# An attention and feed-forward layer: turning blocks of 32 by 32 on VectorE instead of whole tiles on TensorE

## The reference

```
q, k, v = split(x @ qkv_w + qkv_b)
local   = softmax over the 128 keys behind each query (q . k / 4) @ v      # per head
pooled  = x averaged over chunks of 8 tokens (64 chunks)
rq, (rk, rv) = x @ rq_w + rq_b, split(pooled @ rkv_w + rkv_b)              # 4 heads of 16
lat_out = softmax over earlier chunks (rq . rk / 4) @ rv
remote  = lat_out @ rout_w + rout_b                                        # 256 wide, 16 heads of 16
gate    = sigmoid(local @ gl_w + remote @ gr_w)                            # one number per token and head
mixed   = gate * local + (1 - gate) * remote
x1      = layernorm(x + mixed @ out_w + out_b)
xn      = x1 / (rms(x1) + 1e-8);  h = gelu(xn @ ternary(w_up).T)
out     = layernorm(x1 + h / (rms(h) + 1e-8) @ ternary(w_down).T)
```

## Time and profile before

| | us |
|---|---|
| three runs | 1149.62, 1155.28 (median), 1156.93 |
| profiled execution | 1154.15 |
| its span, first to last instruction | 1152.4 |
| busy: TensorE, VectorE, POOL, ScalarE | 1019.2, 902.5, 698.0, 682.4 |

### The profile page before, as it was taken

How to read it: one execution, slowest core, us unless ns; L and a number is a source line. 1 busy time by engine, 2 the same in 40 slices (tenths; PEclk the granted TensorE clock), 3 DMA queues, 4 the chain that set the end, 5 groups by cost and what they waited for, 6 DMA issues and landing times.

```text
span 1152.4 us, 37627 instructions
## 1 busy us (share of the span) xinstructions
PE 1019.2 (88%) x15616; PEld 642.4 (56%) x15616; DVE 902.5 (78%) x2119; ACT 682.4 (59%) x1076; POOL 698.0 (61%) x874
## 2 busy tenths in 40 slices
PE   5878999999999999999999999999999999986855
PEld 2445565655556565655656565565656555564533
DVE  6688888887887988787888888788788878875445
ACT  2425666656666665666666565666666566664523
POOL 7216675656667576566757565566756565673744
PEclk9889999999999999999999999999999999996877
DMA  7740604325060423416061331616042250600000
GB/s 219 204 125 14 193 21 120 87 77 148 32 193 23 145 61 104 121 42 182 24 167 56 113 94 59 166 33 187 28 131 77 85 139 33 174 23 20 2 19 18
DMA packets 46662, 108.18 MB, mean 94 GB/s; under 512 B 7542, under 2 KB 26486, under 8 KB 43382
## 3 DMA queue, kind: packets, MB, share of 16 engines
q1 hardware_dynamic: 46348, 105.78, 31.9%
q10 hardware_dynamic: 144, 0.00, 0.0%
HBM read 71.58 MB, written 34.08 MB: 92 GB/s over the span
## 4 chain that ended last, share of the span: by engine, by line
PE 44%; DVE 28%; ACT 16%; issue 5%; POOL 3%; DMA 2%; SPq 1%; DVEq 0%; POOLq 0%; ACTq 0%
PE oacc L1459 8%; PE work L1537 7%; PE oacc L1480 6%; PE work L1398 5%; PE scores L1439 4%; ACT Pt L792 4%; PE work L1469 3%; DVE Pt L974 3%; DVE nmax L1048 3%; DVE x L1111 2%; DVE rem L1115 2%; PE scores L1377 2%; ACT hbuf L828 2%; PE work L1403 2%; DVE oT L1176 2%
## 5 line engine op out<-in xcount | busy, mean ns | idle before, releaser
L792 ACT ACTIVATE Pt<-scores 128x1024 f32<-128x1024 f32 (+1 forms) x256 | 228.6, 915 | 104.5 <-PE oacc L1459 63.8
L1048 DVE TENSOR_REDUCE nmax<-work 128x3 f32<-128x480 f32 x352 | 218.1, 637 | 25.2 <-PE work L1403 20.0
L656 POOL TENSOR_TENSOR h_lo<-hbuf,h_hi 128x512 f16<-128x512 f32 x128 | 148.2, 1158 | 130.7 <-DVE h_hi L1170 130.7
L628 POOL TENSOR_SCALAR_AFFINE_SELECT Pt<-Pt 128x512 f32<-128x512 f32 x256 | 166.8, 652 | 91.2 <-ACT Pt L792 90.0
L615 POOL TENSOR_TENSOR parts<-Pt,parts 128x512 bf16<-128x512 f32 x64 | 72.9, 1157 | 138.2 <-ACT parts L728 138.2
L1459 PE MATMUL oacc<-Pt,Vp 128*32 128x256 f32 (+1 forms) x2048 | 150.2, 360 | 5.8 <-DVE ytok L1192 2.7
L1398 PE MATMUL work<-Ks,Qs 98*32 98x160 bf16 x4096 | 139.8, 235 | 11.4 <-DVE nmax L1048 7.4
L1439 PE MATMUL scores<-Qs,Ks 100*32 100x160 bf16 (+4 forms) x4096 | 114.8, 230 | 23.5 <-ACT Pt L792 15.9
L1480 PE MATMUL oacc<-wdn_t,h_hi 128*128 128x256 f16 x512 | 118.2, 273 | 5.6 <-POOL h_lo L656 5.6
L632 POOL TENSOR_SCALAR_AFFINE_SELECT Pt<-Pt 128x512 f32<-128x512 f32 x192 | 122.0, 635 | 0.0
L1297 PE MATMUL scores<-xT,wqk 128*128 128x512 f32 x256 | 114.9, 602 | 6.1 <-DMA xT<-x_t 6.1
(11 more groups left out here) (158 smaller groups left out, 1952.9 us busy)
## 6 DMA issues: line engine op xcount, KB each, us to landing
parts_scratch<-parts SPq DMA_DIRECT2D x96, 256.0 KB, 4.5
Qs<-parts_scratch SPq DMA_DIRECT2D x96, 256.0 KB, 4.7
Ks<-parts_scratch SPq DMA_DIRECT2D x96, 256.0 KB, 4.9
xT<-x_t SPq DMA_DIRECT2D x16, 512.0 KB, 6.6
xres<-x SPq DMA_DIRECT2D x16, 512.0 KB, 7.2
y<-ytok SPq DMA_DIRECT2D x16, 512.0 KB, 3.4
nat<-up_t SPq DMA_DIRECT2D x1, 1024.0 KB, 9.6
nat<-down_t SPq DMA_DIRECT2D x1, 1024.0 KB, 11.8
```

The lines of the kernel that those rows point to most:

```text
L628: ins = pool.affine_select(out=pt[:, :, 0:P], in_=pt[:, :, 0:P], compare_op=ALU.is_gt, fill=0.0, base=0, pattern=[[0, 4], [1, P]], channel ...
L656: pool.tensor_tensor(h_lo[:, t % NR, :], hbuf[:, t % 2, :], h_hi[:, t % NR, :], ALU.subtract).then_inc(h_lo_ready, 1)
L792: nc.scalar.activation(Pt[:, u % NPT, :, 0:w], scores[:, slot, :, :].rearrange("p k (h q) -> p (k h) q", h=2)[:, :, 0:w], ACT.Exp, scale=S ...
L1048: nc.vector.tensor_reduce(nmax[:, :, :].rearrange("p b h -> p (b h)")[:, first:first + n], work[:, slot, 0:n * BAND].rearrange("p (h c) -> ...
```

## The change

VectorE turns 32 by 32 blocks itself. A head group in `oacc` goes in one transpose from PSUM into o_q, 32 tokens on the partitions of each of four quadrants, so the copy by ScalarE, the TensorE transpose and a bank of `work` are gone. Gate, mix and remote part take the same layout: the remote part is computed transposed (channels on partitions), drained by ScalarE with its bias (remT, remgT) and turned by VectorE into rem and remg; the gate's remote term comes from a product of its own with the folded matrix wrog. The gate uses tanh: sigmoid(z) = (1 + tanh(z/2))/2. The mix is done in two halves of 512 columns; POOL takes the remote products, and VectorE turns the sum into mixT, so MIX_T is gone. The rows of rout_w and out_w are laid out to fit. The maxima are turned and split by VectorE alone (`split_maxima`) and go straight into Qs by 16 small transfers, ahead of the output store on SP.

Both output products now stand behind all query-key products and the latent query product, one behind the other. The chunk sums are formed one sequence earlier, behind UP + 6, and x_t is loaded one sequence earlier. The last normalisation moves from VectorE (first half) to ScalarE (around GATE, `normalise_before`), y2 lies in the staging buffer `nat`, and POOL's root step of the first norm also gives the inverse root, so VectorE's reciprocal for it (L1154) goes.

The diff, cut to its core; the layouts of the weights, new buffers and semaphores are left out:

```diff
-GATE, MIX_T, OUT, NORM, XN_T, XN_HI, XN_LO, UP = 0, 1, 2, 4, 6, 8, 9, 10
+GATE, OUT, NORM, XN_T, XN_HI, XN_LO, UP = 0, 1, 3, 5, 7, 8, 9
-    ("F", GATE), ("P", QK), ("P", QK + 1), ("P", QK + 2), ("P", QK + 3), ("F", MIX_T),
-    ("P", LAT_RQ), ("F", OUT), ("P", LAT_RKV), ("F", OUT + 1), ("P", VALUES), ("P", LAT_SCORES), ("F", NORM),
+    ("F", GATE), ("P", QK), ("P", QK + 1), ("P", QK + 2), ("P", QK + 3), ("P", LAT_RQ),
+    ("F", OUT), ("F", OUT + 1), ("P", LAT_RKV), ("P", VALUES), ("P", LAT_SCORES), ("F", NORM),
...
+POOL_AT = ("F", UP + 6)
+NORMALISE_AT = {("F", GATE): (0, 1), ("P", QK + 2): (2, 3)}
...
-            order.append(("O", i, (u - 7) // NB))
-        order += [("T", i + 1, t) for t in range(2) if u == T_AT[t] and i + 1 < B]
...
+                wait_alone(sp, nmax_split, count(s, 1, 0))
+                for j in range(2):
+                    row = Qs[s.par][MAXR + j:MAXR + j + 1, :, :].rearrange("a h n -> a (h n)").rearrange(
+                        "a (k r w) -> a k r w", k=2, w=P)
+                    for g in range(NG):
+                        quadrant = slice(g * GT, (g + 1) * GT)
+                        for k in range(2):
+                            sp.dma_start(row[:, k, :, quadrant], nmax_pair[quadrant, j, k * GT:(k + 1) * GT]
+                                         ).then_inc(nmax_in[s.par], 16)
...
+                            pool.wait_ge(gate_ng, count(s, 1, 0))
+                        of_half = rem[:, s.par, :, i * G32 // 2:(i + 1) * G32 // 2, :].rearrange(
+                            "p t b (m d) -> p t (b m) d", m=2)
+                        ng = gate[:, 2, :, i * G32 // 2:(i + 1) * G32 // 2, :].rearrange("p t b m -> p t (b m)")
+                        pool.tensor_tensor(of_half, of_half, ng.unsqueeze(3).to_broadcast([P, KT, G32, HD]),
+                                           ALU.mult).then_inc(mix_part, 1)
...
+                        act.wait_ge(rem_turned, count(s, 2, -1))
+                    for i in range(2):
+                        bank, n = p_use(s, R_REM + i)
+                        act.wait_ge(p_full[bank], n + 1)
+                        for t in range(KT):
+                            ins = nc.scalar.activation(remT[:, t, i * HALF:(i + 1) * HALF],
+                                                       p_bank(bank)[:, t * HALF:(t + 1) * HALF], ACT.Identity,
+                                                       bias=brem[:, t:t + 1])
+                        ins.then_inc(p_taken[bank], 1)
+                    act.wait_ge(p_taken[bank], n + 1)
+                    act.sem_inc(rem_copied, 1)
...
+            def normalise_before(s, b):
+
+                if b == 0:
+                    act.wait_ge(fin_ready, count(s, 1, -1))
+                nc.scalar.activation(y2[:, b, :], y2[:, b, :], ACT.Identity, scale=fin[:, 0, b:b + 1],
+                                     bias=fin[:, 1, b:b + 1]).then_inc(y_ready, 1)
...
-                if k == QK + 1:
-                    dve.wait_ge(x_in[s.par], (s.half + 1) * 16)
...
-                if REMOTE <= k < REMOTE + NB // 2:
-                    for b in (k - REMOTE, k - REMOTE + NB // 2):
-                        bank, n = take(R_REM + b)
-                        nc.vector.tensor_tensor(rem[:, s.par, b, :], p_bank(bank)[:, 0:RW], brem[:, :], ALU.add
-                                                ).then_inc(p_taken[bank], 1)
+                if k == REMOTE:
+                    dve.wait_ge(rem_copied, count(s, 2, 0))
+                    for t in range(KT):
+                        ins = nc.vector.transpose(rem[:, s.par, t, :, :].rearrange("p b d -> p (b d)"), remT[:, t, :])
+                    ins.then_inc(rem_turned, 1)
...
+                nc.vector.transpose(nmaxT[:, :], nmax[:, :]).then_inc(nmax_vec, 1)
+                dve.wait_ge(nmax_vec, count(s, 2, 0))
+                nc.vector.tensor_copy(nmax_pair[:, 0, :], nmaxT[:, :]).then_inc(nmax_vec, 1)
+                dve.wait_ge(nmax_vec, count(s, 2, 1))
+                nc.vector.tensor_tensor(nmax_pair[:, 1, :], nmaxT[:, :], nmax_pair[:, 0, :], ALU.subtract
+                                        ).then_inc(nmax_split, 1)
...
-                nc.vector.tensor_copy(
-                    o_tok[:, :, 4 * hg:4 * hg + 4, :],
-                    work[:, slot, :].rearrange("p (b h d) -> p b h d", b=NB, h=4)[:, :, :, 0:VW]
-                ).then_inc(w_taken[slot], 1)
+                dve.wait_ge(pv_done, count(s, NU, NB * hg + NB - 1))
+                nc.vector.transpose(o_q[:, hg // 2, :, hg % 2, :],
+                                    oacc[:, hg % 2, :].rearrange("p (b d) -> p b d", d=GT)).then_inc(o_taken, 1)
...
+                    done(nc.vector.tensor_tensor(a, of_heads[:, :, VN],
+                                                 dead[:, :, :, :].rearrange("p t b m -> p (t b m)"), ALU.add))
+                    done(nc.vector.reciprocal(r, a))
+                    done(nc.vector.tensor_tensor(a, of_heads[:, :, HD], r, ALU.mult))
+                    dve.wait_ge(rem_turned, count(s, 2, 1))
+                    for t in range(KT):
+                        of_t = [gate[:, j, t, :, :].rearrange("p (i b) m -> p i b m", i=2) for j in (0, 4)]
+                        remote = remg[:, s.par, :, :].rearrange("p b (i r) -> p i b r", i=2)
+                        ins = nc.vector.tensor_tensor(of_t[0], of_t[1], remote[:, :, :, 2 * t:2 * t + 2], ALU.add)
+                    ins.then_inc(gate_z, 1)
+                    mark(nc.vector.tensor_scalar(half_r, r, 0.5, None, ALU.mult))
...
+                    nc.vector.tensor_scalar(ng, e, -0.5, 0.5, ALU.mult, ALU.add).then_inc(gate_ng, 1)
+                    sync()
+                    done(nc.vector.scalar_tensor_tensor(out=a, in0=e, scalar=1.0, in1=half_r,
+                                                        op0=ALU.add, op1=ALU.mult))
...
+                    for i in range(2):
+                        mark(nc.vector.tensor_tensor(
+                            mixed[:, i, :, :].rearrange("p t (k d) -> p t k d", d=HD),
+                            of_half(o_q, i)[:, :, :, :, 0:HD].rearrange("p t b m d -> p t (b m) d"),
+                            of_half(gate[:, 4, :, :, :], i).rearrange("p t b m -> p t (b m)").unsqueeze(3
+                                ).to_broadcast([P, KT, G32, HD]), ALU.mult))
+                    sync()
+                    for i in range(2):
+                        dve.wait_ge(mix_part, count(s, 2, i))
+                        done(nc.vector.tensor_tensor(mixed[:, i, :, :], mixed[:, i, :, :],
+                                                     of_half(rem[:, s.par, :, :, :], i).rearrange(
+                                                         "p t b d -> p t (b d)"), ALU.add))
+                        nc.vector.transpose(mixT[:, i, :, :].rearrange("p t n -> p (t n)"),
+                                            mixed[:, i, :, :].rearrange("p t n -> p (t n)")).then_inc(mixT_in, 1)
...
+                    if (phase, k) == POOL_AT and s.third_next().exists:
+                        pool_chunks(s.third_next())
...
+                    banks = [bank_p(s, R_REM + i) for i in range(2)]
+                    for t in range(KT):
+                        for i in range(2):
+                            rows = slice(i * LD, (i + 1) * LD)
+                            mm = nc.tensor.matmul(p_bank(banks[i])[:, t * HALF:(t + 1) * HALF],
+                                                  wro[rows, t * P:(t + 1) * P], lat_oT[rows, :], start=True, stop=True)
+                            if t == KT - 1:
+                                mm.then_inc(p_full[banks[i]], 1)
+                if k == REMOTE + 1:
+
+                    bank = bank_p(s, R_REM + 2)
+                    nc.tensor.matmul(p_bank(bank)[:, 0:HALF], wrog[:, :], lat_oT[:, :], start=True, stop=True
+                                     ).then_inc(p_full[bank], 1)
```

More of the change, by code:

```diff
@@ L799, in f_step @@
                     act.wait_ge(gate_z, count(s, 1, 0))
[L800 removed]
+                    nc.scalar.activation(gate[:, 1, :, :, :], gate[:, 0, :, :, :], ACT.Tanh, scale=0.5
                                          ).then_inc(gate_e, 1)
[L802 to L805 removed]
                 if NORM <= k < NORM + 2:
@@ L1231, in body @@
                         ternary_down((2, 5, 8).index(u))
-                    if not s.last:
-                        for t in range(2):
-                            if u == T_AT[t]:
-                                max_low(s.next(), t)
+                    if u == A_STEPS and not s.last:
+                        split_maxima(s.next())
                 later = s.second_next()
```

368 lines of the change are left out of this document (169 added, 199 removed).

## The result

| | us |
|---|---|
| before, median of 4 runs | 1154.97 |
| changed, median of 4 runs (1196.49 to 1205.14) | 1201.30 |
| ratio, 95% interval | 1.0407, [1.035, 1.0463] |
| profiled execution's span, before and changed | 1152.4, 1196.8 |
| mean granted clock, before and changed | 0.965, 0.932 |

The change makes the kernel 4% slower; the forecast was 1119, its range 1100 to 1150. The 44.4 us between the two spans lie as follows, read from the first write of y2 in each sequence: 14.2 up to the first one (165.57 against 151.36), 34.0 in the next fourteen periods (68.6 each against 66.2), -4.5 in the last period (59.98 against 64.44), 0.7 behind it.

The account below looks back on a forecast made before the run. VectorE's queue was taken to set the second half, with TensorE, VectorE and POOL near full in the attention stretch. 1154.15 - 34 (periods) - 5.5 (tail) + 3.5 (start) = 1118.2, 1119 against the median; range 1100 to 1150.

Parts of the forecast that it names:

- two products of 512 columns, done at 4.35, while POOL does the remote products: In the mix: VectorE's two products run from t = 3.05 to 4.35, POOL's remote ones from 2.85 to 5.15.
- a stall of 0.65: TensorE's latent query product, behind the query-key products, waits 0.65 us for the bank VectorE's first qk_rest frees at 7.7.
- the output products run from 8.75 to 12.55: On TensorE in the second half, behind the latent query product: output products take from t = 8.75 to 12.55.
- the first gelu: End of the chain from the last attention product: first gelu moves from t = 24.04 to 21.5, gain 2.5 a period.
- -34: Sum over fourteen periods, in us: -2.5 second half, +1.2 period's end, -1.1 attention stretch, -2.4 each.
- the start: Ahead of the first attention stretch, VectorE waits for sequence 2's chunk sums: +3.5 us, between +2.5 and +7.
- the tail: Sequences 14 and 15: -5.5 us (-3 to -7), from -4.5 for sequence 15's mix and +0.5 for the last normalisation.
- the transpose's price: VectorE's transpose of 512 columns takes 0.68 us; scaling the Trainium skill's figure by columns would give 1.24.
- rival 1: Slow transposes: 1.36 us for 512 columns on VectorE, a period loses 2.4 us, 1189 in all; chance 10%.
- rival 3: POOL late with the remote products, 2.3 us each, so the mix ends 1.75 later; 1143 in all; chance 12%.
- The attention stretch: Stretch of 22.58 us with three engines near full: gain 1.1 us a period, between 0 and 1.8, to 21.5.
- The end: Period's end: remote part and chunk sums on VectorE delay h_sum and the squares' product, loss 1.2 us a period.

Follow-up runs that it names:

- experiment 1: Changed kernel with POOL's two remote products of the mix made by VectorE behind its own two: 1182.48 us, ratio 1.0222.
- experiment 2: Changed kernel with POOL's remote products started only when VectorE's own two are done: 1215.58 us, ratio 1.0519.
- experiment 12: kernel 9 with the two remote products back on POOL beside VectorE's own two: 1118.60 us, ratio 0.9674.
- experiment 7: Kernel of experiment 1 with POOL's four additions of the output bias moved behind the mix: 1167.53 us, ratio 1.0099.
- experiment 11: Changed kernel with three useless TensorE products filling the wait ahead of the latent query product: 1182.26 us, ratio 1.0222.
- experiment 4: Changed kernel with the split maxima sent through DRAM by five issues instead of 16 direct ones: 1196.06 us, ratio 1.0318.
- experiment 5: Changed kernel with three start edits: tiny POOL instruction behind the all-reduce, sequence 2's x_t ahead of the maxima, its chunk sums ahead of the last turns: 1192.37 us.
- experiment 8: Changed kernel with mix on VectorE half by half, output products ahead of latent query product, bias additions moved, end and start rearranged, maxima through DRAM: 1148.55 us.
- kernel 9: Kernel of experiment 8 with VectorE's remote-part turns spread behind later feed-forward blocks and POOL's last two query-key parts behind the first norm's x1: 1112.05 us.

## Why the prediction was wrong, step by step

*The step that failed first* is "two products of 512 columns, done at 4.35, while POOL does the remote products". Each engine was priced alone, 0.65 and 1.157, and the overlap was taken for free. Alone they do take 0.65 and 1.03; together the means are 1.49 and 1.26, because the two engines' instructions run one after the other. Experiments 1, 2 and 12 show it from three sides. Two more places in the same half have the same cause: POOL's bias additions (2.77) now run beside the gate's short passes, because the gate starts at t = 1.03, where it stood at 1.92 (the mix's products start at 3.64 instead of the forecast's 3.05; with the additions moved, in experiment 7, they start at 3.05), and VectorE's L1211, two columns wide, takes 1.10 beside a POOL part where the same line takes 0.15 beside the roots. With that and roots of 1.34 instead of 1.02 (six columns for four, since the root now gives the inverse too, which the prediction left at no cost), the last scale comes 1.3 later still.

The Trainium skill (SBUF — State Buffer, section "Who interferes with whom") states that a VectorE instruction with two inputs in SBUF contends with a POOL instruction that reads SBUF, and that one with at most one such input, outside certain fast modes, does not. The runs agree: the products, the adds and the gate's first sum are held up, while h_sum, with one operand in PSUM, takes 0.68 beside POOL's h_lo. Its word that whoever starts first keeps the port and the loser blocks fully is what is seen: POOL's first product is not slowed, and the four run in turn, 3.07 from the first start to the last end, against 1.29 + 2.06 one after the other. One row does not fit: L1211, with two operands in SBUF, takes 0.15 at 547.78, inside POOL's root of 547.15 to 548.48.

The trace of before could have told me as well, and on the mix itself. In sequence 0 POOL's pause put its bias additions beside the mix, and the same passes over 256 columns went from 0.42 to 0.95, POOL's four from 2.8 to 3.53:

```profile
110.41 0.42 DVE L1111 TENSOR_TENSOR x<-o_tok,gate 128x256 f32<-128x256 f32 x1
110.74 0.95 DVE L1115 TENSOR_TENSOR rem<-rem,gate 128x256 f32<-128x256 f32 x1
```

```profile
110.47 3.53 POOL L681 TENSOR_TENSOR xres<-xres,bout 128x256 f32<-128x256 f32 x4 [7.43 <-issue]
```

A cast has one operand and is held up too, in every sequence. One stands ahead of POOL's h_lo, the other starts inside it (534.17 to 535.33):

```profile
531.02 0.43 DVE L1170 CAST h_hi<-hbuf 128x512 f16<-128x512 f32 x1
...
534.62 1.00 DVE L1170 CAST h_hi<-hbuf 128x512 f16<-128x512 f32 x1
```

*The second step* is "a stall of 0.65" for the latent query product and "the output products run from 8.75 to 12.55". The stall's mechanism was right; with the mix 2.35 late it became 2.95, and I had given the pause no price in clock. It cost 0.9 on the latent query product and 0.6 on the output products here, and 19 us in all (experiment 11). The drop does not always start at once: in three of the thirteen periods the latent query product still took 1.08, and the output products behind it 5.4 instead of 3.72.

The ledger of the first gelu in sequence 7, 26.35 against 21.5: 0.6 gate, 1.7 products, 1.4 clock, 1.3 roots and scales, sum 5.0 (4.85 measured). Fourteen times 4.85 is 68, about the distance from -34 to +34; by the median, 26.55, it would be 71, but the measured distance also holds before's longer mean (66.2, where the forecast used 66.02) and a shorter last period of the fourteen (67.3). With 10.7 more at the start (14.2 for 3.5) and 1.7 more in the tail (-3.8 for -5.5) this is the whole miss of 80 us of span.

*Right*: the transpose's price, 0.705 against 0.68; the estimate of 1.24 does not hold, and rival 1's cause is false (its sign came true by another mechanism, which none of my rivals named; rival 3 had POOL's product late, not the two engines holding each other up). The attention stretch, 21.55 against 21.5, though at a clock of 0.92 (median of the periods 21.4). The end: first gelu to h_sum's end takes 18.39 (to 573.33), before 16.98, a loss of 1.4 against 1.2. The last period, -4.5, is right by luck: all of it was to come from the mix in sequence 15's second half, which gave 3.0 (its mix stands at t = 9.33, not 7.05), and 1.5 came from the attention stretch ahead of it. One row was misread: "no VectorE row shown here takes over 1.65 ns a column" holds for the wide passes, not for L1100, 64 columns in 0.56.

*The start* was to cost 3.5 and cost 14.2. The first maxima come at 89.30, 8.5 late, where 83.5 was forecast and +7 the bound. The step named for it, x_t behind SP's sixteen transfers, is only a small part: they took 0.63 each (rows 6 give up to 0.67, 4.00 for six, not 0.61), but VectorE waits only 1.38 for x_t. In experiment 4, with five transfers, that wait is gone and the maxima still come at 89.03 (its prologue ran 1.2 later); in experiment 5, with x_t early and the chunk sums ahead, at 86.49. What the forecast left out is the remote part's new chain in the prologue. TensorE waits 3.00 for VectorE at 50.64, the prologue is 3.9 late at 77.72 (the weights' pass L977, 73.78 before), and then VectorE waits 3.75 for ScalarE's drains before it can turn them. How the 3.9 divide was not tested. The other 6 is POOL's pause, which stands in before's trace and had become a wait by moving work to POOL; I costed a moved step without its new queue. Experiments 1 and 5 show this part. In sequence 14 TensorE waits 11.81 for the rows, where I had them land 1 us later than for the 3.85 of before: experiment 4 prices it at 5.5, and the tail that was to be -5.5 kept little but the last period's -4.5.

*Open*: what starts the low clock in some attention stretches (0.92 in the changed kernel, 0.87 in experiment 8) and not in others was not isolated.

Repaired, the change is worth what was forecast, but not by the forecast's sum: kernel 9's period is 63.5 where 63.6 was predicted, and its time 1112 where 1119 was, with the mix wholly on VectorE, the first gelu at 22.5 instead of 21.5, and h_sum's end 16.4 behind it instead of 18.2, since the remote products and their drains left that stretch. That the totals agree is in part luck.

## What to carry to other kernels

Work handed to POOL so that VectorE can do its own share meanwhile can win only if VectorE's instructions then have at most one operand in SBUF and are no casts, or POOL's reads fall elsewhere; here four products on VectorE took 2.5, two there and two on POOL 3.1. Look in the old trace for one operation of VectorE with two durations, in the first sequence too, and see what POOL did in each. Put a product whose input is late behind one whose input is there; TensorE's pause costs its length and the slow clock behind it. And a step moved to another engine inherits everything in that engine's queue, start-up pauses included.

## What the runs showed of the hardware

- VectorE's 32 by 32 transpose of 512 f32 columns takes 0.705 from PSUM and 0.711 from SBUF, and was not slowed beside POOL (0.70 at 528.88, beside a bias addition); 256 columns take 0.43, 64 take 0.205.
- Of two f32 products with both operands in SBUF, one on VectorE and one on POOL, the one that starts second waits for the other: 512 columns on VectorE 0.65 alone and 1.52 to 1.54 behind POOL, on POOL 1.06 when first and 1.51 when second.
- A pause of 2.95 of TensorE was followed by products at a granted clock of 0.50, 1.2 GHz, at once or within the next products; with 2.74 of filling work the products behind ran at 1.00, 2.4 GHz.
- POOL stood still 7.4 to 8.4 ahead of its first tensor_tensor behind a partition_all_reduce, at both places tried: at 111 to 119, with masks in between, and right behind it at 53 to 62.
- Sixteen SBUF to SBUF transfers of 32 runs of 64 bytes occupy SP 10.02, 0.63 each.
